# A two-layer graph kernel on one core: row sums kept by left and right half, and turned on VectorE in 32x32 blocks instead of on TensorE

## What is computed

```python
def L0(x, adj, u):
    keep = (u >= 0.1).astype(x.dtype)
    return jnp.matmul(adj, x * keep / (1.0 - 0.1))

def L1(x, adj, weight, bias):
    return jnp.matmul(adj, jnp.matmul(x, weight)) + bias

x = _layernorm(x + L0(x, adj, u), axis=-1)
x = _layernorm(x + L1(x, adj, weight, bias), axis=-1)
```

## Time and profile before

| | us |
|---|---|
| median of 3 runs | 902.91 (902.78 to 903.06) |
| the profiled execution, its own time | 902.77 |
| its span, first to last instruction | 901.0 |
| PE busy | 873.1 (97%) |
| DVE busy | 529.6 (59%) |
| ACT, POOL busy | 30.2, 25.3 |
| DMA | 359.60 MB, mean 399 GB/s, queue 1 at 96.7% of 16 engines |

### The profile page before, as it was taken

One profiled execution on the slowest core, in us unless ns is written; L12 is line 12 of the kernel. 1 busy time (PEld: TensorE's weight loads), 2 busy tenths in 40 slices (PEclk: granted clock), 3 DMA queues, 4 the chain that ended last, 5 costly groups with the idle time before them and its releaser, 6 DMA issues.

```text
span 901.0 us, 13601 instructions
## 1 busy us (share of the span) xinstructions
PE 873.1 (97%) x5754; PEld 406.1 (45%) x5754; DVE 529.6 (59%) x1026; ACT 30.2 (3%) x74; POOL 25.3 (3%) x24
## 2 busy tenths in 40 slices
PE   3899999999999999999999999999999999999996
PEld 3653333333343444535354554636446456456343
DVE  6356123126145656766676667768677768768655
ACT  0100000000000000000000000000000000000011
POOL 3000000000000000000000000000000000000133
PEclk9999999999999999999999999999999999999998
DMA  9999999999999999999999999989899999999952
GB/s 373 411 416 421 420 420 420 421 421 420 420 420 422 419 420 420 420 401 410 420 420 403 413 404 380 422 352 422 359 408 419 414 417 419 420 421 419 420 242 71
DMA packets 55404, 359.60 MB, mean 399 GB/s; under 512 B 6448, under 2 KB 10544, under 8 KB 12592
## 3 DMA queue, kind: packets, MB, share of 16 engines
q1 hardware_dynamic: 55344, 358.74, 96.7%
HBM read 356.61 MB, written 2.10 MB: 398 GB/s over the span
## 4 chain that ended last, share of the span: by engine, by line
PE 92%; DMA 4%; SPq 2%; issue 1%; DVE 1%; POOLq 0%; POOL 0%; ACT 0%; DVEq 0%
PE psum L996 22%; PE psum L949 21%; PE psum L964 8%; PE psum L931 8%; PE psum L958 8%; PE psum L982 6%; PE psum L917 5%; PE psum L938 4%; PE psum L1002 4%; DMA tiles<-adj_chunks 2%; DMA tiles<-adj_t 2%; PE psum L894 1%; SPq L495 1%; PE psum L1017 1%; PE psum L1032 1%
## 5 line engine op out<-in xcount | busy, mean ns | idle before, releaser
L949 PE MATMUL psum<-tiles,stat 128*64 128x512 f32 x976 | 216.8, 593 | 0.1
L996 PE MATMUL psum<-tiles,stat 128*64 128x512 f32 x944 | 211.7, 594 | 0.0
L656 DVE TENSOR_TENSOR layer<-psum,layer 128x512 f32<-128x512 f32 (+1 forms) x143 | 98.6, 689 | 182.8 <-PE psum L996 85.6
L949 PEld LDWEIGHTS psum<-tiles,stat 128*64 128x64 f32 x976 | 69.6, 137 | 128.2 <-issue 122.5
L996 PEld LDWEIGHTS psum<-tiles,stat 128*64 128x64 f32 x944 | 66.5, 137 | 123.7 <-issue 121.4
L692 DVE TENSOR_TENSOR tiles<-tiles 128x512 f32<-128x512 f32 x90 | 62.2, 691 | 53.7 <-PE psum L940 51.7
L966 PE MATMUL psum<-tiles,stat 128*64 128x256 f32 x360 | 92.7, 380 | 0.0
L933 PE MATMUL psum<-tiles,stat 128*64 128x256 f32 x360 | 92.4, 379 | 0.0
L931 PE MATMUL psum<-tiles,stat 128*64 128x256 f32 x360 | 92.4, 379 | 0.0
L931 PEld LDWEIGHTS psum<-tiles,stat 128*64 128x64 f32 x360 | 49.3, 137 | 40.9 <-issue 20.0
L680 DVE TENSOR_TENSOR tiles<-tiles 128x512 f32<-128x512 f32 x90 | 60.6, 683 | 10.0 <-DMA tiles<-adj_t 10.0
(11 more groups left out here) (100 smaller groups left out, 849.5 us busy)
## 6 DMA issues: line engine op xcount, KB each, us to landing
tiles<-adj_t SPq DMA_DIRECT2D x306, 1024.0 KB, 13.4
tiles<-adj SPq DMA_DIRECT2D x12, 1024.0 KB, 19.2
tiles<-adj_chunks SPq DMA_DIRECT2D x12, 1024.0 KB, 20.4
tiles<-xu SPq DMA_DIRECT2D x4, 1024.0 KB, 7.9
tiles<-adj_parts SPq DMA_DIRECT2D x16, 256.0 KB, 17.7
x_res<-x SPq DMA_DIRECT2D x16, 128.0 KB, 13.9
out<-layer SPq DMA_DIRECT2D x8, 256.0 KB, 2.1
w<-weight SPq DMA_DIRECT2D x4, 16.0 KB, 9.6
```

The costliest lines, as they stand in the source:

```text
L656: return dve.tensor_tensor(out=to, in0=addend, in1=to, op=ALU.add)
L949: last = pe.matmul(sum_f[i % 2][to, :], stat[:, j * C + c, 0:D], tile[:, c], start=begun.get("f") != i and c < 2, stop=ends and c >= 2, sk ...
L996: last = pe.matmul(bank[to, :], stat[:, j * C + c, D:2 * D], tile[:, c], start=c == 0, stop=c == C - 1)
```

## The change

- The sum of a row is kept in another way. Each `first` job is now 8 matmuls of 256 columns: for each piece c, `low` takes the left 256 columns and `high` the right 256, with the same weights. So `sum_f` holds the whole sum, left half of the nodes in partitions 0 to 63 and right half in 64 to 127, in 256 columns.
- `turn` is no longer a job. At `row_end` DVE adds layer 1's part in two 64x256 operations (rows 2 and up), turns the 128x256 block with one `transpose` in 32x32 blocks into `turned`, and adds x in 16 operations of 32 partitions by 2x32 values, since each 32x32 block comes out in its own place. Then it normalises as before; `sum_stat` follows, and `centre_weights` now comes after h of row 14.
- ACT's copy and PE's four transposes of each of the 15 rows are gone. The first row, done in four parts, is turned as before (`turn_part`).
- In the list of jobs of rows 1 to 3 some `chunk` and `early` jobs come at other places; the tile jobs of rows 4 to 15 keep their order.

```diff
-            if pieces and (i > 1 or len(filler) % 2 == 0):
+            if pieces and (len(filler) == ECHO_BANKS if i > 1 else len(filler) % 2 == 0):
...
-                jobs.append(("turn", i - 1) if i > 1 else ("part_turn", PARTS - 1))
+                if i == 1:
+                    jobs.append(("part_turn", PARTS - 1))
...
-    jobs += again[:1]
-    jobs.append(("turn", NB - 1))
-    jobs += again[1:]
+    jobs += again
...
-                    act.activation(halves[other, :], sum_f[i % 2][other, :], ACT.Copy).then_inc(half_by_act, 1)
...
+            def turn(i):
+                k = turns(i) - 1
+                dve.wait_ge(s_res[i % 2], 16 * (i // 2 + 1))
+                dve.wait_ge(h_ready, k)
+                source = sum_f[i % 2] if i < EARLY else halves
+                last = dve.transpose(turned[:, 0:B // 2], source[:, 0:B // 2])
+                if i < EARLY:
+                    last.then_inc(half_by_dve, 1)
+                    dve.wait_ge(half_by_dve, turns(i))
+                else:
+                    step(last)
+                t = turned[:, 0:B // 2].rearrange("p (c e f) -> p c e f", c=2, f=QUAD)
+                x_rows = x_res[:, i % 2].rearrange("p (c d) -> p c d", c=C)
+                for side in range(2):
+                    c = slice(2 * side, 2 * side + 2)
+                    for features in range(2):
+                        f = slice(features * QUAD, (features + 1) * QUAD)
+                        at = slice((2 * side + features) * QUAD, (2 * side + features + 1) * QUAD)
+                        for e in range(C):
+                            to = slice(e * QUAD, (e + 1) * QUAD)
+                            last = dve.scalar_tensor_tensor(out=r[to, c, f], in0=t[at, :, e], scalar=KEPT,
+                                                            in1=x_rows[to, c, f], op0=ALU.mult, op1=ALU.add)
+                            if (side, features, e) != (1, 1, C - 1):
+                                last.then_inc(dve_step, 1)
...
+                normalise(i, slice(0, C))
+                if EARLY <= i < NB - 2:
+                    sum_stat(i)
+                if i == NB - 2:
+                    centre_weights()
...
-                        dve.tensor_tensor(out=halves[of_row(i), :], in0=sum_f[i % 2][of_row(i), :],
-                                          in1=layer1_pair(i)[of_row(i), :], op=ALU.add).then_inc(half_by_dve, 1)
+                        own = layer1_pair(i)[of_row(i), :]
+                        step(dve.tensor_tensor(out=halves[0:D, 0:B // 2], in0=sum_f[i % 2][0:D, 0:B // 2],
+                                               in1=own[:, 0:B // 2], op=ALU.add))
+                        dve.tensor_tensor(out=halves[D:P, 0:B // 2], in0=sum_f[i % 2][D:P, 0:B // 2],
+                                          in1=own[:, B // 2:B], op=ALU.add).then_inc(half_by_dve, 1)
+                        dve.wait_ge(half_by_dve, turns(i))
+                    turn(i)
...
-                            to = low if c % 2 == 0 else high
-                            last = pe.matmul(sum_f[i % 2][to, :], stat[:, j * C + c, 0:D], tile[:, c],
-                                             start=begun.get("f") != i and c < 2, stop=ends and c >= 2,
-                                             skip_group_check=True)
+                            for to, columns in (low, left), (high, right):
+                                last = pe.matmul(sum_f[i % 2][to, left], stat[:, j * C + c, 0:D], tile[:, c, columns],
+                                                 start=begun.get("f") != i and c == 0, stop=ends and c == C - 1,
+                                                 skip_group_check=True)
```

More of the change, by code:

```diff
@@ L34 @@
 C = 4
+QUAD = 32
 B = C * P
@@ L319, in resnorm_graph_layers @@
     for job in jobs:
-        if job[0] in ("row_end", "turn"):
+        if job[0] == "row_end":
             chain_at = done_after[job]
@@ L1010, in _ @@
                               start=True, stop=True).then_inc(scale_summed, 1)
-                elif kind == "turn":
-                    i = job[1]
-                    pe.wait_ge(turned_read, turns(i) - 1)
-                    pe.wait_ge(half_by_act, turns(i))
-                    pe.wait_ge(half_by_dve, turns(i))
-                    for c in range(C):
-                        last = pe.transpose(turned[:, c * P:(c + 1) * P], halves[:, c * P:(c + 1) * P], ident[:, :])
-                    last.then_inc(turned_ready, 1)
                 elif kind == "final":
```

56 lines of the change are left out of this document (25 added, 31 removed).

## The result

The kernel with the change takes 909.92 us, the median of 4 runs (909.10 to 910.75), where the kernel before, run beside it, takes 902.98. The ratio is 1.0079, 95% interval 1.0067 to 1.0091: 0.8% slower. The forecast was 906.4 in a range of 902.8 to 911. The direction was right and the mechanism was the one named, but the size was short by 3.5 us.

What follows compares the result with a forecast made beforehand. PE was taken to bound the kernel behind the tile landing at 287.54 us. The sum was 902.77 - 7.9 (turns gone) + 0.9 (cut matmuls) + 10.6 (new waits for DVE's joins) = 906.4 us, range 902.8 to 911.

Steps and rivals of the forecast that it cites:

- rivals 2 and 4: DVE's transpose takes 0.84 us, total 909.8; or PE's cut matmuls are bound by weight loads; together 908.5 to 913, chance 0.12.
- PE is the bound behind 287.54: After the tile landing at 287.54 us, a microsecond less on PE is one less in all, absent new waits.
- a turn is worth 0.74: Each row-end turn removed from PE saves 0.74 us; eleven turns, row 5 counted at 0.5, save 7.9 us.
- An operation that goes to other partitions waits for the last one's end, 0.254 a step: DVE's sixteen additions at a row's end each wait for the one before: 0.254 us each, 4.06 us.
- The transpose, 0.45 with its wait: DVE's 128x256 transpose at a row's end, estimated from nearby operations, takes 0.45 us including its wait.
- The waits, 10.6: PE waits for DVE's join behind eight rows (7, 9 to 15), 0.89 to 3.1 us each, 10.6 us together.
- may add some tenths: PE restarting after each of eight waits may add some tenths of a microsecond, not counted in the 906.4.
- The cut matmuls, 0.015 a job: Cutting PE's 512-column matmuls in two costs 0.015 us a job, 0.9 us over 62 jobs behind 287.54.
- The early stretch costs nothing: Turns of rows 1 to 4 and moved jobs of rows 1 to 3 count nothing, hidden by transfers before 287.54.
- the first: DVE's sixteen additions overlap at a 0.14 us step, so most PE waits vanish: 897.1 us, faster; chance 0.16.
- the third: Margins just meet: DVE's chain 0.3 to 0.45 shorter, or transfers bound later rows; 902.9 to 904, no change; chance 0.12.
- the fourth: PE's cut matmuls are bound by weight loads, every percent on 62 jobs 1 us; chance 0.12 shared with a slow transpose.

Runs made afterwards that it cites:

- x_moves: Changed kernel with its sixteen additions writing partitions 0 to 31 of a separate buffer, only the x read changing partitions: 907.12 us, ratio 1.0047.
- read_moves: Changed kernel with its sixteen additions writing partitions 0 to 31 of a separate buffer, only the PSUM read changing partitions: 910.09 us, ratio 1.0081.
- same_place: Changed kernel with all sixteen additions reading partitions 0 to 31 and writing partitions 0 to 31 of a separate buffer: 898.51 us, ratio 0.9951.
- split_late: Kernel before, transposes kept, with the first jobs' matmuls cut in two in rows 7 to 15 alone: 903.18 us, ratio 1.0004.
- split_12: Kernel before, transposes kept, with the first jobs' matmuls cut in two in rows 1 and 2 alone: 902.77 us, ratio 1.0000.
- old_rule: Changed kernel with the kernel before's rule for where the pieces of rows 1 to 3 go: 915.08 us, ratio 1.0137.
- after_again: The changed kernel run again with nothing altered, beside the other kernels of a later job: 909.68 us.

## Why the prediction was right, and where it was short

- **The number.** 909.92 lies in the stated range, but in the band from 908.5 to 913, to which I had given 0.12 and which stood for a slow transpose or costly cut matmuls (rivals 2 and 4). Neither came out. What carried the time there is 1.1 us of waits, 1.9 of late tiles and 0.7 of the clock, and the last two were not in the forecast; that the range reached to 911 was luck as far as they go.
- **PE is the bound behind 287.54, and a turn is worth 0.74.** Right: 0.73 in each of eleven rows. The 0.2 that I took off row 5, as lying in the stretch bound by transfers, was not needed.
- **An operation that goes to other partitions waits for the last one's end, 0.254 a step.** Right, 0.25, and the term on which the sign hangs: with 0.13 the kernel takes 898.5. My reading of the earlier trace rows against the earlier trace rows carried it, and `x_moves` and `read_moves` bear it out for reads. The Trainium skill's rule (page "VectorE: DVE Perf Modes", section "Two Vector instructions with no wait between them") agrees with all four kernels: by it the sixteen are held in the changed kernel, `read_moves` and `x_moves`, and free in `same_place`.
- **The transpose, 0.45 with its wait.** Measured 0.46, and 0.50 from its start to its follower's. Rival 2 is out.
- **The waits, 10.6.** The places and their order are right, all eight and no other; the sum is 11.7. In row 10 the terms were: DVE's first operation 0.30 behind PE's (I had 0.38), the chain 5.50 (5.49), from L605 to the join 4.70 (4.58), and from the join's end to PE's matmul 549.11 - 548.96 = 0.15 where I had 0.05. The hand-over and the join's place are the terms that were mis-sized. The hand-over took 0.15 in all eight waits. The join's place is the held join of the section on moved operands, 0.12 in row 10: from L605 to it `same_place` and `x_moves` have 4.58, as the kernel before has. I had used the rule for the additions and not for the join behind them. The note that a restart "may add some tenths" pointed at it without a number.
- **The cut matmuls, 0.015 a job.** The changed kernel's trace gives 0.012 (0.75 for 62), the median of `split_late` 0.008. It was 0.2 to 0.4 us too much in all.
- **The early stretch costs nothing.** Wrong, in the step "The turns of rows 1 to 4, and the jobs that changed places in rows 1 to 3, lie ahead of the tile of 287.54; I count them at nothing". What PE does there in time is hidden, as `split_12` shows. But the number of PE's instructions there sets when its code is read, and with the read that makes the gap in the stretch bound by transfers the last tiles came 1.7 us later, 1.4 of it in that gap. The forecast looked only at how long PE takes, not at what PE's longer code adds to the transfers. I had also put the end of the bound stretch at 287.54, while PE waits for tiles up to 324 us once they are 1 us later.
- **The clock.** Missed. At the wait of 2.6 to 2.9 us in row 14 the granted clock sometimes falls to the lower of its two levels, 1.2 for 2.4 GHz. PE at the end of row 14 in the changed kernel, where it is not, then in `read_moves`, where it is, with the granted clock of 790 to 796 us there:

```profile
789.61 1.94 PE L1035 MATMUL psum<-tiles,stat 128*64 128x512 f32 x8 [2.85 <-DVE layer L649]
```

```profile
789.23 3.31 PE L1038 MATMUL psum<-tiles,stat 128*64 128x512 f32 x8 [2.79 <-DVE layer L650]
```

```profile
790.00:796.00 6.00, 6.00 (x26) 2.17 (x24) 2.65 (x4) 0.00 (x0) 0.00 (x0) 0.83 1.01 422
```

  The same eight matmuls take 3.31 for 1.94, 1.4 us more. `old_rule` shows the same (3.41, in the section on it), and so does `x_moves`, whose row 14 and granted clock from 786 to 790 us are:

```profile
787.89 3.48 PE L1039 MATMUL psum<-tiles,stat 128*64 128x512 f32 x8 [2.60 <-DVE layer L650]
791.09 3.87 PE L1033 MATMUL psum<-tiles,stat 128*64 128x512 f32 x16
```

```profile
786.00:790.00 4.00, 2.11 (x6) 0.83 (x8) 3.65 (x10) 0.00 (x0) 0.00 (x0) 0.77 1.01 426
```

  Against the changed kernel (1.94 for the eight, 3.63 for the sixteen) these lose 1.5 and 0.2 us, and this execution of `x_moves` took 1.6 to 1.9 us longer than the other three. The changed kernel's two slower executions are 1.4 to 1.7 above the other two. That they are this case is likely, but no trace of one is there, and the mean clock of an execution (0.994 for 0.998) does not show it: the kernel before has means from 0.995 to 0.998 at the same time. It would account for the 0.7 between the median and the profiled execution.

Of the rivals, the first has been made to happen (`same_place`), the third came out in none, and the fourth, cut matmuls bound by weight loads, is kept small by the trace: 0.75 us for all 62 jobs, 0.7%.

## What to carry to other kernels

Before moving a piece of work from the bound engine to a helper, look at what stood between its pieces: the join between DVE's copy and its turn was the slack that let PE run on, and putting one join back turns 0.8% lost into 0.4% won. Small operations on one engine cost by their step and not by their own time, so lay them out such that neighbours keep to the same partitions, look also at the larger operation that follows them, or share them with an idle engine. Where transfers are the bound, the number of instructions of an engine is a cost too, even where its time is hidden: here one gap of 1.0 to 1.8 us to eight reads of PE's code, some 2000 instructions (an estimate, 8 x 256).

## What the runs showed of the hardware that I had not expected

- A read of PE's code on queue 8 (16 KB, 1.07 us, one to about 256 instructions) puts back one of a tile's 16 shares. In a saturated stream one read in eight meets a share that is already the last and makes a gap of 1.0 to 1.8 us: the 9th and the 17th, or in `old_rule`, whose stream had stood still in between, the 9th, the 12th and the 20th. ACT's code goes by queue 14, and twice as much of it left the time as it was (902.83 for 902.88).
- An operation of 64 values a partition takes about 0.20 to 0.22 us on DVE, but the next can start 0.13 after it when all operands stay in their 32 partitions, and 0.24 to 0.25 after it when one read moves, in PSUM or in SBUF. The join, a read of PSUM from partition 0 on, starts 0.21 behind the operation before it, or 0.32 to 0.33 when the last read of PSUM was of partitions 96 to 127.
- ACT copies 32x64 from PSUM, with the output moving, at (1.82 us for eight) 0.23 a step.
- After an idle of 6.39 us PE's granted clock was 0.50 of 2.4 GHz from 140 to 143 us, the lower level of 1.2 GHz; in row 14, at waits of 2.60, 2.79 and 2.83 us, it fell in three traces (`x_moves`, `read_moves`, `old_rule`), and at waits of 2.84 and 2.85 us, in the two traces of the changed kernel (`after_again` is the second), it did not.
